# Latent attention: where VectorE adds a turn's result to the residual

## What is computed

```python
def _L1_xattn_ref(x, latents, mask, ...):          # x: the context, latents: layernorm of the residual
    xn = layernorm(x, ln_x_g, ln_x_b)
    ln = layernorm(latents, ln_l_g, ln_l_b)
    q = (ln @ Wq).reshape(b, m, h, d).transpose(0, 2, 1, 3)
    kv = jnp.concatenate([xn @ Wkv, ln @ Wkv], axis=1)
    ...
    qn = rmsnorm(q, qn_g) * scale
    kn = rmsnorm(k, kn_g)
    sim = jnp.einsum('bhid,bhjd->bhij', qn, kn)
    ...
    attn = jax.nn.softmax(sim.astype(jnp.float32), axis=-1).astype(sim.dtype)
    out = jnp.einsum('bhij,bhjd->bhid', attn, v)
    out = out.transpose(0, 2, 1, 3).reshape(b, m, h * d)
    return out @ Wout + bout

x = x + _L1_xattn_ref(ctx_1024, _layernorm(x, axis=-1), ...)
```

## Time and profile before

| | before |
|---|---|
| median of three runs | 2029.51 us |
| profiled execution | 2032.73 us |
| its span | 2031.0 us |
| TensorE busy | 1838.8 us (91%) |
| VectorE busy | 1459.9 us (72%) |
| ScalarE busy | 978.2 us (48%) |
| GpSimd busy | 770.9 us (38%) |

### The profile page before, as it was taken

How to read it: one execution, slowest core, us unless ns; L and a number is a source line. 1 busy time by engine, 2 the same in 40 slices (tenths; PEclk the granted TensorE clock), 3 DMA queues, 4 the chain that set the end, 5 groups by cost and what they waited for, 6 DMA issues and landing times. The chain is left out here.

```text
span 2031.0 us, 30630 instructions
## 1 busy us (share of the span) xinstructions
PE 1838.8 (91%) x10970; PEld 1255.0 (62%) x10970; DVE 1459.9 (72%) x2771; ACT 978.2 (48%) x1461; POOL 770.9 (38%) x622
## 2 busy tenths in 40 slices
PE   4988999679999999999978999779689999989898
PEld 2556888444444444445435777545458889957797
DVE  6676897767677776777757888799699955667533
ACT  2555888445666666666634555345300210045443
POOL 2332322156777676767661344243211301012010
PEclk8997999779999999999998999889899999989799
DMA  1000311100000000000000212000000110000000
GB/s 63 1 0 14 116 63 53 50 1 1 1 1 1 1 1 1 1 1 1 1 19 0 91 66 73 12 1 0 17 16 21 32 52 0 7 5 0 6 21 32
DMA packets 19323, 42.80 MB, mean 21 GB/s; under 512 B 3236, under 2 KB 10937, under 8 KB 16902
## 3 DMA queue, kind: packets, MB, share of 16 engines
q1 hardware_dynamic: 18742, 41.07, 6.0%
q10 hardware_dynamic: 464, 0.20, 0.0%
HBM read 40.09 MB, written 1.18 MB: 20 GB/s over the span
## 5 line engine op out<-in xcount | busy, mean ns | idle before, releaser
L1770 POOL TENSOR_TENSOR sb_L_total<-sb_L_total,sb_L_probT 128x512 f32<-128x512 f32 (+1 forms) x192 | 268.3, 1421 | 50.1 <-ACT sb_L_probT L2074 46.5
L395 POOL TENSOR_TENSOR sb_L_prob<-sb_L_prob,sb_L_rsum 128x616 f32<-128x616 f32 (+1 forms) x96 | 98.2, 1045 | 272.0 <-DVE sb_L_rsum L637 272.0
L2074 ACT ACTIVATE sb_L_probT<-banks 128x1024 f32<-128x1024 f32 x128 | 131.2, 1025 | 135.6 <-PE banks L1903 135.1
L2131 DVE TENSOR_REDUCE sb_L_top_tok<-banks 128x2 f32<-128x1024 f32 x128 | 155.9, 1220 | 24.1 <-PE banks L1870 23.9
L1913 PE MATMUL banks<-sb_L_probT,sb_L_v 128*64 128x512 f32 x512 | 137.6, 616 | 0.2 <-DVE sb_L_mixedT L2182 0.2
L1767 POOL TENSOR_TENSOR sb_L_total<-sb_L_probT 128x512 f32<-128x512 f32 x64 | 80.8, 1285 | 126.1 <-ACT sb_L_probT L2074 126.1
L543 ACT ACTIVATE sb_L_probT<-banks 77x512 f32<-77x512 f32 x160 | 89.8, 590 | 76.8 <-PE banks L446 76.8
L2495 DVE SCALAR_TENSOR_TENSOR sb_L2f_hid<-banks,sb_L2f_weight,sb_L2f_hid 128x512 f32<-128x512 f32 x176 | 122.4, 745 | 2.5 <-PE banks L97 1.6
L2565 DVE SCALAR_TENSOR_TENSOR sb_resid<-banks,sb_L2f_weight,sb_resid 128x128 f32<-128x128 f32 x192 | 67.2, 351 | 62.5 <-PE banks L97 57.8
L1478 DVE TENSOR_TENSOR sb_L0f_hid_low<-sb_L0f_raw,sb_L0f_hid_high 128x1024 fp32r<-128x1024 f32 x64 | 86.4, 1368 | 28.4 <-ACT sb_L0f_hid_high L1435 28.1
L432 PE MATMUL banks<-sb_L_kdiag,sb_L_qT 128*128 (+2 forms) x192 | 84.3, 580 | 21.2 <-DVE sb_L_prob L628 10.1
(11 more groups left out here) (403 smaller groups left out, 5113.6 us busy)
## 6 DMA issues: line engine op xcount, KB each, us to landing
sb_L0f_wide<-spread_L0f SPq DMA_DIRECT2D x8, 1024.0 KB, 6.1
sb_L1f_wide<-spread_L1f SPq DMA_DIRECT2D x8, 1024.0 KB, 6.3
sb_fetched<-L2f_w SPq DMA_DIRECT2D x12, 256.0 KB, 2.6
sb_fetched<-L1f_gu SPq DMA_DIRECT2D x8, 336.0 KB, 3.0
sb_fetched<-L0f_w SPq DMA_DIRECT2D x8, 259.0 KB, 2.7
sb_fetched<-L0f_w SPq DMA_DIRECT2D x8, 256.0 KB, 3.2
sb_normT<-L2f_w SPq DMA_DIRECT2D x2, 768.0 KB, 4.8
sb_L2f_hid<-L2f_w SPq DMA_DIRECT2D x2, 768.0 KB, 5.0
```

The source lines that it names most:

```text
L395: pool.tensor_tensor(grid, grid, bcast(rsum[:, i % PROBS, half], [None, KEYS]), ALU.mult).then_inc(normed, 1)
L1770: pool.tensor_tensor(sums[rows], sums[rows], probT[rows, k, h], ALU.add).then_inc(added[h], 1)
L2074: act.activation(probT[:, k], ps[:, slot:slot + 2, :], ACT.Exp).then_inc(exped, 1)
L2131: dve.tensor_reduce(top_tok[:, :, k:k + 1].rearrange("p h k -> p (h k)"), ps[:, banks:banks + 2, :], AX.X, ALU.max).then_inc(bound_read, 1)
```

## The change

In VectorE's list, at the end of a turn, `add_result(turn - 1)`, and the one wait of turn 1 that stands ahead of it, move in front of `low_queries(turn + 2)` (and of `norm.part` in turn 0, where there is nothing to add). No instruction is added or removed, and no other engine's list changes.

```diff
@@ -2241,14 +2241,14 @@
                         high_queries(turn + 2)
                     if more:
                         take_lead(turn + 1)
+                    if turn == 1:
+                        dve.wait_ge(bias_added, 1)
+                    if turn > 0:
+                        add_result(turn - 1)
                     if much:
                         low_queries(turn + 2)
                     if turn == 0:
                         norm.part(dve, 3)
-                    if turn == 1:
-                        dve.wait_ge(bias_added, 1)
-                    if turn > 0:
-                        add_result(turn - 1)
                     if turn == TURNS - 2:
                         wait_read(dve, Y, turn - 1)
                         nxt.norm.moments(dve, 0, 2)
```

## The result

Over 20 runs of each kernel the median was 2024.44 us after the change and 2030.31 us before, a ratio of 0.9969 with a 95% interval of 0.996 to 0.9977. By that ratio the change is 6.3 us faster, between 4.7 and 8.1 (the two medians differ by 5.9). One of the 20 runs after the change took 4329.63 us, for a reason that nothing recorded shows, and is left out of the ratio. I had forecast 2030.8 us, 1.3 us slower, which is no change that a measurement could tell.

The account below looks back on a forecast made before the run. TensorE was taken as the bound, busy 596.7 of 620 us. Terms 4.8 + 2.0 - 0.4 - 4.4 - 0.7 gave +1.3 us on the 2029.5 us median: 2030.8 us, range 2018.5 to 2035.0.

Parts of the forecast that it names:

- The addition, 11.0 us off TensorE's wait: Before L1870: the addition, moved ahead, ends before the keys' product, so the gap vanishes in 22 places, 11.0 us.
- GpSimd holds the low part up, not the order on VectorE: At the turn's end: GpSimd's hold on the shared SBUF port lengthens the low part from 0.675 to 1.162 us.
- The low part comes behind the sum in the 14 turns with turn % 4 of 3 or 0 and in 25 and 29, and waits it out: At those turns' ends: low part takes 1.81 us, delaying NKL by 0.32 us; +4.8 us over 15 turns.
- Rival 1: At the turn's end: the low part wins the port, 2023.7 or 2018.8 us; chance 0.17.
- a median of the low part under 1.2 us: Sign in the low part's line durations that would prove the port claim wrong; about 1.8 us was expected.
- It is free in turns 1, 5, ... 21: At those turns' ends: GpSimd's last sum is over at 542.52, so the low part, starting at 542.50, takes 0.68 us.
- For turn 1: At NKL in turn 1: it starts 2.85 us behind the keys' product instead of 3.29, -0.4 us.
- Turns 2, 6, ... 26: Low part meets a sum midway, 1.32 us; NKL 3.13 us behind the keys' product, now 2.85; +2.0 us.
- The encounter in turns 5 to 21 ends, -4.4 us: In turns 5, 9, 13, 17, 21: L2135 no longer loses a whole GpSimd sum; 5 x -0.9 us.
- rival 4: In turns 4, 8, ... 28: late NKL makes L2135 lose to a sum; +7.7 us, 2038.5 us; chance 0.13.
- The sum of the turns: All turns' terms: 4.8 + 2.0 - 0.4 - 4.4, with -0.7 for turn 30 giving +1.3 us.
- The tail, -0.7 us: Turn 30: its bound waits 1.4 us and gets the addition 1.1 us earlier; -0.7 us, between 0 and -1.1.

Follow-up runs that it names:

- the port free: GpSimd's fifth-chunk sum cut to one column, in the kernel before and the changed kernel: 523.2 and 523.3 us from lead 2 to lead 29.
- second profile: The changed kernel run and profiled once more, nothing altered: ratio 0.9966 against the kernel before, median 2024.34 us.
- made to lose: Changed kernel, but the low part waits for the addition's end: ratio 1.0003 against the kernel before, median 2030.52 us.
- made to win: Changed kernel, but the addition of turns 0 to 28 covers three of four token tiles: ratio 0.9934 against the kernel before, median 2016.78 us.
- the mixed order: Changed kernel, but turns with turn % 4 = 2 keep the old order: ratio 0.9953 against the kernel before, median 2021.49 us.

## Why the prediction was wrong, step by step

- *The addition, 11.0 us off TensorE's wait*: right, 11.0 to 0.3 us, and L1870 follows K in every turn.
- *GpSimd holds the low part up, not the order on VectorE*: right. With the port free the orders are equal to 0.1 us.
- *The low part comes behind the sum in the 14 turns with turn % 4 of 3 or 0 and in 25 and 29, and waits it out*: this step failed. The distances were right, 0.01 to 0.03 us, and so was the price of a lost tie (1.81 us, NKL at K + 3.61; expected 1.81 and 3.62). But I took an order of two recorded starts, 0.02 us apart, for a decision. The rows that I had read could have warned me: of two L2135 that came 0.01 and 0.02 us ahead of a sum one lost and one came through the earlier trace rows. In the two profiles of the changed kernel the low part won 20 of 42 such ties. Rival 1, which I gave 0.17, had all ties won; I never thought of a draw for each turn. Per turn a win was worth 0.67 us. The sign that I had named for this, a median of the low part under 1.2 us, did not show it (1.32 us in both profiles), since seven turns lie between the won and the lost ones.
- *It is free in turns 1, 5, ... 21*: wrong in effect. I took GpSimd's list there from turns that had the encounter; as the encounter goes, the lead comes 1.2 us earlier against GpSimd's list, and these turns become near ties too (turns 5 and 21 lost, 9, 13 and 17 won in the first profile). I had counted their own NKL as if lost in turns 5 to 21, so the sum did not suffer by it there. For turn 1 I had counted a win, -0.4 us; it was lost in both profiles, and from lead 1 to lead 2 the changed kernel took 20.9 us instead of 20.6, +0.3.
- *Turns 2, 6, ... 26*: right, 1.31 to 1.33 us and K + 3.11 to 3.13, expected 1.32 and 3.13.
- *The encounter in turns 5 to 21 ends, -4.4 us*: right. In the kernel with all ties lost these five turns took 19.85 us instead of 20.75, 5 x 0.9 = 4.5 us, and in the changed kernel 19.2 to 19.85. (The 0.9 us is 1.2 for the encounter less 0.3 for a lost tie; I had 1.1 and 0.23.) What I had not seen is that L2171 may meet a sum anew, as in turns 16 and 24 of the second profile, 1.2 us each; this is near to rival 4, which I gave 0.13.
- *The sum of the turns*: with all ties lost I had 4.8 + 2.0 - 4.4 = +2.4 us; the kernel made to lose showed +1.4 over the stretch. The 15 lost turns cost 0.27 us each there instead of 0.32. Its whole time, 2030.5 us and a ratio of 1.0003 (0.9993 to 1.0013), agrees with the +1.3 us that I forecast, though by parts that differ from mine, in the tail above all. The change made 532.6 us of the 538.35 by winning nine ties within the stretch. That its time comes near rival 1's 2023.7 us is luck: about half of the ties were won, and with all of them won (made to win) the kernel took 2016.8.
- *The tail, -0.7 us*: mis-sized. It gave 2.6 us (17.5 to 14.9), because I priced the wait and not TensorE's clock behind it. Without the fall of the clock the same wait makes 16.0 us of the turn, and with the new order and a lost tie it takes 15.15, 0.8 less, about what I had; the clock's 1.5 us stood nowhere in the sum.

So of the 6.3 us, 4.3 (536.9 less 532.6) come from the turns and 2.6 from the tail; together 6.9, and with the 0.3 us lost behind turn 1 6.6, within the interval. The 2.7 us by which the profiled executions also differ between the leads of turns 0 and 1 lie ahead of the first moved step that could matter there. TensorE is at half its clock for a while in turn 1 in four of the six traces with the old order and in two of the eight with the new one (in every turn, or in all but each fourth). The stretch follows a wait of TensorE for the last part of the norm (L95), which no edit was aimed at: in ten of the fourteen traces this wait has 2.8 to 3.1 us, and the clock falls behind it in six of them, of both orders; where it has 1.3 to 2.1 us, in four, it does not. So the same wait is followed by the fall in one run and not in the next. The kernel before and the changed kernel, the wait and TensorE's clock behind it (timeline and windows):

```profile
440.68 0.48 PE L95 MATMUL banks<-sb_norm_high,sb_L_w_low 128*128 128x512 f32 x1 [2.79 <-DVE sb_norm_low L294]
...
442.10:445.50 3.40, 3.40 (x12) 1.49 (x14) 2.07 (x3) 1.15 (x2) 0.00 (x0) 0.50 0.00 0
```

```profile
440.30 0.47 PE L95 MATMUL banks<-sb_norm_high,sb_L_w_low 128*128 128x512 f32 x1 [2.79 <-DVE sb_norm_low L294]
...
441.70:445.10 3.40, 3.35 (x18) 1.45 (x20) 3.11 (x4) 2.38 (x4) 0.15 (x1) 1.00 0.00 0
```

I have no mechanism by which a moved step that comes behind it could do that, and whether the order has a part in it stays open.

## What to carry to other kernels

Where VectorE and GpSimd both work on SBUF, a reordering on one of them moves it against the other's list, and what it gains in waits can be lost or won there: look at each moved instruction with two inputs in SBUF and ask which GpSimd instruction is running when it comes. If two starts are within some hundredths of a microsecond, the order in one profile settles nothing: price both outcomes (here 29 of 63 ties were won), or move the step to where its wait is covered; here the low part in an idle stretch of the next turn was worth more than the forecast change. And price a long wait of TensorE by the clock that follows it as well.

## What the runs showed of the hardware

- Between a VectorE instruction that reads two SBUF operands and a GpSimd sum, a start 0.01 to 0.03 us behind the other's recorded start does not settle who is served first: 20 of 42 won in the two profiles of the changed kernel, 9 of 21 in the mixed order, and more of those at 7 to 18 ns (23 of 38) than at 19 to 24 ns (6 of 25). At 0.13 us behind (made to lose: 1.31 us behind the lead, the sum at 1.18) none of the 21 turns from 3 to 29 in which they meet so was won; at 0.11 us ahead (made to win: 1.07 us, the sum at 1.18) all 21 from 1 to 29 in which they meet were.
- The loser waits until the other is over, rather than running beside it more slowly: the low part takes 1.81 us when it loses at the start of a sum, 1.32 us when it comes half a microsecond into one, and 0.67 us without a rival; the sum takes 1.83 us when it loses, 1.29 us without.
- A single wait of TensorE of 1.4 us, in a stage in which it is otherwise 96% busy, was followed in three of four traces by a stretch at half clock, which cost about 1.5 us (17.5 against 16.0 for the turn). A wait of 0.9 us at the same place was not followed by one (one trace). A wait of 2.8 to 3.1 us in turn 1 was in six of ten.
